# Mamba block with expert gate on one core: another way to the layer-norm roots in the first stage, another order at its start

## What is computed

```python
def _layernorm(x, axis=-1, eps=1e-05):
    m = jnp.mean(x, axis=axis, keepdims=True)
    v = jnp.var(x, axis=axis, keepdims=True)
    return (x - m) / jnp.sqrt(v + eps)
...
xn = _layernorm(x)
x = xn @ Wx.T
z = xn @ Wz.T
x = jax.nn.silu(_causal_conv(x, conv_w, conv_b))
b, c = x @ Wb.T, x @ Wc.T
dt = jax.nn.softplus(x @ Wdt.T + b_dt)
y = _ssd_scan(x, b, c, dt, a) + d_param * x
s = (groupnorm(y) * silu(z)) @ Wout.T
g = silu(experts(xn))          # router: softmax(xn @ Wr + br), top 1024 tokens of each expert
out = x_input + s * g
```

## Time and profile before

| | us |
|---|---|
| median of 3 runs | 1302.14 (1301.19 to 1302.91) |
| the profiled execution | 1301.87 |
| its span, first to last instruction | 1300.1 |

### The profile page before, as it was taken

The page is one execution under the profiler, slowest core; times in us unless marked ns, Lnnn a source line. Parts: engine busy times, 40 slices in busy tenths (PEclk is TensorE's granted clock), DMA queues, the critical chain, the costliest instruction groups (busy, mean ns, idle before and its releaser), DMA issues.

```text
span 1300.1 us, 26491 instructions
## 1 busy us (share of the span) xinstructions
PE 1267.4 (97%) x10300; PEld 1058.3 (81%) x10300; DVE 935.5 (72%) x1877; ACT 634.7 (49%) x1302; POOL 775.8 (60%) x685
## 2 busy tenths in 40 slices
PE   6889999999999999999999999899999999999999
PEld 4556667888888888888888887699899989899998
DVE  7888676777756567567667657798677766787786
ACT  5888996433444443334333443444343332555554
POOL 3778865434444565567666545456666654577774
PEclk9999899999999999999999999899999999999999
DMA  8465355743544344354444444375454545777884
GB/s 280 141 240 209 124 211 171 149 147 135 155 146 166 128 133 155 134 173 138 149 137 154 139 147 143 131 209 114 91 115 88 97 87 117 224 256 255 267 267 155
DMA packets 121276, 210.55 MB, mean 162 GB/s; under 512 B 18368, under 2 KB 91712, under 8 KB 112832
## 3 DMA queue, kind: packets, MB, share of 16 engines
q1 hardware_dynamic: 107568, 191.67, 45.2%
q0 software_dynamic: 12288, 17.05, 7.7%
q10 hardware_dynamic: 1296, 0.15, 0.1%
HBM read 140.93 MB, written 67.90 MB: 161 GB/s over the span
## 4 chain that ended last, share of the span: by engine, by line
PE 81%; POOL 6%; DVE 5%; issue 3%; ACT 3%; DMA 2%; SPq 0%; POOLq 0%; ACTq 0%; DVEq 0%
PE ps L1125 22%; PE ps L1464 10%; PE ps L1721 9%; PE ps L1944 7%; PE ps L1923 7%; PE ps L1180 4%; PE ps L1249 4%; PE ps L527 2%; PE ps L1261 2%; PE ps L1212 2%; POOL acc L479 2%; PE ps L1195 2%; PE ps L1229 2%; PE ps L569 2%; DVE acc L227 1%
## 5 line engine op out<-in xcount | busy, mean ns | idle before, releaser
L1092 ACT ACTIVATE decay<-tap,ncum 128x128 f32<-128x128 f32 x344 | 105.4, 389 | 144.7 <-POOL tap L1005 144.5
L1649 POOL DMA_INDIRECT ffn_dram<-ob,idx x64 | 109.8, 1716 | 83.1 <-DVE ob L1568 68.8
L1683 ACT ACTIVATE mid<-ps,b_up 128x512 f32<-128x512 f32 x96 | 65.9, 688 | 154.3 <-PE ps L1464 152.5
L1034 POOL TENSOR_SCALAR yb<-x,dcol 128x512 f32<-128x512 f32 x64 | 45.2, 708 | 154.4 <-DMA y_dram<-yb 96.1
L924 DVE TENSOR_TENSOR yb<-ps,yb 128x256 f32<-128x256 f32 x128 | 48.4, 420 | 123.0 <-PE ps L1261 118.9
L1011 POOL TENSOR_TENSOR x_lo<-x,x_hi 128x512 fp32r<-128x512 f32 x56 | 75.0, 1340 | 81.0 <-ACT x_hi L1078 80.9
L1022 POOL TENSOR_TENSOR c_dec<-cT,ecum_row 128x512 f32<-128x512 f32 x64 | 87.1, 1361 | 34.0 <-PE ps L1261 23.8
L479 POOL TENSOR_TENSOR acc<-acc,tap 128x512 f32<-128x512 f32 x64 | 82.0, 1286 | 36.4 <-DVE acc L227 35.5
L1125 PE MATMUL ps<-x_hi,w_hi_c 128*128 128x512 f32 x240 | 99.6, 415 | 0.0
L1125 PE MATMUL ps<-x_hi,w_hi_b 128*128 128x512 f32 x240 | 99.5, 415 | 0.0
L1806 POOL TENSOR_SCALAR yc<-yc,gn_scale,gn_shift 128x512 f32<-128x512 f32 x56 | 88.2, 1587 | 16.6 <-DMA yc<-y_dram 16.5
(11 more groups left out here) (305 smaller groups left out, 4070.5 us busy)
## 6 DMA issues: line engine op xcount, KB each, us to landing
tap<-cum_dram SPq DMA_DIRECT2D x43, 512.0 KB, 5.1
x_dram<-x SPq DMA_DIRECT2D x16, 1024.0 KB, 5.1
x<-x_dram SPq DMA_DIRECT2D x16, 1024.0 KB, 6.0
ecum_row<-ecum_dram SPq DMA_DIRECT2D x128, 128.0 KB, 3.0
y_dram<-yb SPq DMA_DIRECT2D x16, 1024.0 KB, 7.5
yc<-y_dram SPq DMA_DIRECT2D x16, 1024.0 KB, 6.2
cum_row<-cum_dram SPq DMA_DIRECT2D x21, 512.0 KB, 5.5
ring<-in_x SPq DMA_DIRECT2D x16, 512.0 KB, 8.1
```

Of the source, the lines that this page charges most:

```text
L1092: n = nc.scalar.activation(decay[g % 2][:, h, :], cum_row[g % NR][:, h, :], ACT.Exp, bias=t.ncum[:, g, h:h + 1])
L1649: pool.indirect_dma_start(out=t.ffn_dram, out_offset=bass.IndirectOffsetOnAxis(ap=t.idx[:, e, h * HC + c:h * HC + c + 1], axis=0), in_=ob[ ...
```

## The change

Six edits, all in the front.

1. **Groups and roots.** The groups become blocks 0, 1, 2, 3, and then 4 to 6, 7 to 9, 10 to 12, 13 to 15. For the first four ACT's Sqrt, DVE's reciprocal and DVE's 4-step `polish` stay, all ahead of ACT's one change to the Silu table. For the others `root` makes the inverse root on DVE alone: a start value by an integer shift, a multiply and an add, then Newton steps, 13 dependent instructions on 128x12 values. Steps 0 to 6 stand at the end of passes 0, 3, 6 and 9, steps 7 to 12 behind `lo_part` in passes 1, 4, 7 and 10. POOL's `polish` and the three late `deviation`s are gone; POOL waits for the 13th step ahead of blocks 4, 7, 10 and 13.
2. **Statistics** run one block less ahead (block b + 6 in pass b, to pass 9).
3. **First loads.** Block 0 comes in two halves; block 1 is issued once the second half has landed; the identity (128 columns of the constants) comes first on ACT's queue, the rest of the constants behind block 1; four small tensors move from ACT's queue to SP's, behind block 7 and ahead of the first store.
4. **Start of the chain.** Block 0 is normalized and turned chunk by chunk (`first_turn`). `deviation(0)` stands ahead of the high part of `wx`, which is made in two halves; DVE makes half of its low part, POOL the other half ahead of block 1. `turn(1)` stands behind all four projections of block 0.
5. **Zeros.** PE runs 26 matmuls on a tile of zeros from the start and 3 more behind `first_turn` (`keep_busy`).
6. DVE, ACT and POOL wait for the late small tensors near the end of the front.

The diff, cut to its core:

```diff
-    GROUPS = ((0, 1), (1, 2), (2, 4), (4, 8), (8, 12), (12, 16))
-    EARLY = 2
+    GROUPS = ((0, 1), (1, 2), (2, 3), (3, 4), (4, 7), (7, 10), (10, 13), (13, 16))
+    EARLY = 4
...
+    WARM, WARM_HI = 26, 3
+    SECOND = (1, 4, 7, 10)
...
                 if c == 0:
                     dve.wait_ge(x_loaded[b % NX], 16 * (b // NX + 1))
+                elif (b, c) == (0, 2):
+                    dve.wait_ge(half_loaded, 16)
                 n = v.bn_stats(stat6[:, CH * b + c, :], xin[b % NX][:, c, :])
                 if c < CH - 1:
...
+            def root(g, first, end):
+                lo, hi = GROUPS[g]
+                n, cols, base = CH * (hi - lo), slice(CH * lo, CH * hi), STEPS * (g - EARLY) + 4 * EARLY + 1 + CH
+                raw, a, y = var[:, 0:n], sq[:, 0:n], rstd[:, cols]
+                for i in range(first, end):
+                    if i == 0:
+                        dve.wait_ge(var_done, hi)
+                        step = v.tensor_scalar(raw, moment[:, cols, 1], EPS, None, ALU.add)
+                    else:
+                        dve.wait_ge(norm_step, base + i)
+                        if i == 1:
+                            step = v.tensor_scalar(a.bitcast(I32), raw.bitcast(I32), 1, None, ALU.arith_shift_right)
+                        elif i == 2:
+                            step = v.tensor_scalar(y.bitcast(I32), a.bitcast(I32), -1.0, float(MAGIC), ALU.mult,
+                                                   ALU.add)
+                        elif i == STEPS - 1:
+                            step = v.scalar_tensor_tensor(nmr[:, cols], moment[:, cols, 0], -1.0, y, ALU.mult,
+                                                          ALU.mult)
+                        elif i % 3 == 0:
+                            step = v.tensor_tensor(a, raw, y, ALU.mult)
+                        elif i % 3 == 1:
+                            step = v.scalar_tensor_tensor(a, a, -0.5, y, ALU.mult, ALU.mult)
+                        else:
+                            step = v.scalar_tensor_tensor(y, a, 1.5, y, ALU.add, ALU.mult)
+                    step.then_inc(norm_step, 1)
...
-                    n = v.tensor_scalar(xn[0][:, c, :], xin[0][:, c, :], rstd[:, c:c + 1], nmr[:, c:c + 1],
-                                        ALU.mult, ALU.add)
-                n.then_inc(xn_ready, 1)
+                    v.tensor_scalar(xn[0][:, c, :], xin[0][:, c, :], rstd[:, c:c + 1], nmr[:, c:c + 1],
+                                    ALU.mult, ALU.add).then_inc(norm_step if c < CH - 1 else xn_ready, 1)
...
+            v.memset(zeros, 0.0)
             v.memset(warm[:, :], EPS).then_inc(norm_step, 1)
             block_stats(0)
             inverse(0)
             polish(0)
...
             dve.wait_ge(wx_hi_done, 1)
-            v.tensor_tensor(wx_lo[:, :, :], wx[:, :, :], wx_hi[:, :, :].bitcast(F32), ALU.subtract).then_inc(
-                wx_lo_done, 1)
-            block_stats(1)
+            v.tensor_tensor(wx_lo[:, 0, :], wx[:, 0, :], wx_hi[:, 0, :].bitcast(F32), ALU.subtract).then_inc(norm_step, 1)
+            stats(1, 0)
...
                 lo_part(0, k)
+            for c in range(1, CH):
+                stats(1, c)
             inverse(1)
             polish(1)
-            block_stats(2)
...
                     conv(b + 1, m)
-                    if m == 1 and b + 2 < NB:
+                    if b == -1 and m in (0, 2):
+                        block_stats(2 + m // 2)
+                        inverse(2 + m // 2)
+                        polish(2 + m // 2)
+                    if m == max(0, min(b + 1, 1)) and b + 2 < NB:
                         for k in range(KT):
                             lo_part(b + 2, k)
-                    if b == -1 and m < 3:
-                        block_stats(3 + m)
-                    elif b == 0 and m < 2:
-                        block_stats(6 + m)
-                    elif b >= 1 and b + 7 < NB:
-                        stats(b + 7, m)
-                    if b == -1 and m == 0:
-                        inverse(2)
-                if b in (0, 4, 8):
-                    inverse(3 + b // 4)
+                        if b in SECOND:
+                            root(EARLY + b // 3, HALFWAY, STEPS)
+                    if b == -1 and m == 3:
+                        block_stats(4)
+                    elif b == 0 and m in (0, 2):
+                        block_stats(5 + m // 2)
+                    elif b >= 1 and b + 6 < NB:
+                        stats(b + 6, m)
+                if b + 1 in SECOND:
+                    root(EARLY + (b + 1) // 3, 0, HALFWAY)
             thin_copy(NB - 2)
             thin_copy(NB - 1)
...
+            act.dma_start(t.ident, ins["const"][:, C_ID:C_ID + P]).then_inc(ident_loaded, 16)
             for dst, src in smalls:
                 act.dma_start(dst, src).then_inc(small_loaded, 16)
...
+            deviation(0)
             act.wait_ge(wx_loaded, 16)
-            nc.scalar.activation(wx_hi[:, :, :], wx[:, :, :], ACT.Copy).then_inc(wx_hi_done, 1)
-            deviation(0)
+            for k in range(KT):
+                nc.scalar.activation(wx_hi[:, k, :], wx[:, k, :], ACT.Copy).then_inc(wx_hi_done, 1)
             for k in range(KT):
                 hi_part(0, k)
-            deviation(1)
...
                 if b == -1:
-                    deviation(2)
+                    deviation(1)
...
+                if b == -1:
+                    split(0, 2)
+                    deviation(2)
                 if b + 2 < NB:
                     for k in range(KT):
...
-                    split(b + 1, 2)
+                    if b >= 0:
+                        split(b + 1, 2)
                     split(b + 1, 3)
+                    if b == -1:
+                        deviation(3)
                 else:
+                    act.wait_ge(late_loaded, 16 * len(lates))
                     nc.scalar.activation(a_pos[:, :, :], t.rows[:, 0:1, :], ACT.Exp).then_inc(sca, 1)
                     thin_evict(b + 1)
...
-                if b in (0, 4, 8):
-                    deviation(3 + b // 4)
...
-            def polish(g):
-                lo, hi = GROUPS[g]
...
-                gp.tensor_scalar(neg[:, 0:n], moment[:, cols, 0], -1.0, 0.0, ALU.mult, ALU.add).then_inc(norm_step, 1)
...
-                pool.wait_ge(norm_step, first + 3)
...
-                pool.wait_ge(norm_step, first + 7)
             def layer_norm(b):
-                if b == 1:
...
+                if b < EARLY:
+                    pool.wait_ge(norm_step, 4 * (b + 1) + 1 + CH)
                 elif b in [lo for lo, _ in GROUPS]:
-                    polish(group_of(b))
+                    pool.wait_ge(norm_step, STEPS * (group_of(b) - EARLY + 1) + 4 * EARLY + 1 + CH)
...
+            pool.wait_ge(wx_hi_done, KT)
+            pool.wait_ge(xn_ready, 1)
+            nc.gpsimd.tensor_tensor(wx_lo[:, 1, :], wx[:, 1, :], wx_hi[:, 1, :].bitcast(F32),
+                                    ALU.subtract).then_inc(wx_lo_done, 1)
             layer_norm(1)
...
+            def keep_busy(n):
+                for _ in range(n):
+                    pe.matmul(ps_x[MT - 1][:, :], zeros[:, 0:P], zeros, start=True, stop=True)
+            def first_turn():
+                for c in range(CH):
+                    pe.wait_ge(*((norm_step, 6 + c) if c < CH - 1 else (xn_ready, 1)))
+                    for k in range(KT):
+                        mm = pe.transpose(ps_t[k][:, c * P:(c + 1) * P], xn[0][:, c, k * P:(k + 1) * P], t.ident)
+                        if c == CH - 1:
+                            mm.then_inc(xnT_ready, 1)
...
-            pe.wait_ge(cst_loaded, 16)
-            turn(0)
-            pe.wait_ge(wx_lo_done, 1)
+            pe.wait_ge(norm_step, 1)
+            keep_busy(WARM)
+            pe.wait_ge(ident_loaded, 16)
+            first_turn()
+            keep_busy(WARM_HI)
             for b in range(-1, NB - 1):
                 project(b + 1, 0)
                 project(b + 1, 1)
-                if b + 2 < NB:
+                if 0 <= b < NB - 2:
                     turn(b + 2)
                 project(b + 1, 2)
                 project(b + 1, 3)
                 if b == -1:
+                    turn(1)
                     pe.wait_ge(small_loaded, 16 * len(smalls))
                 thins(b + 1)
+                if b == 0:
+                    pe.wait_ge(cst_loaded, 16)
                 if b >= 0:
                     sum_thins(b)
...
-            load_x(0)
+            sp.dma_start(xin[0][:, 0:2, :], x_blk[0][:, 0:2, :]).then_inc(x_loaded[0], 16)
+            sp.dma_start(xin[0][:, 2:CH, :], x_blk[0][:, 2:CH, :]).then_inc(half_loaded, 16)
             sp.dma_start(wx[:, :, :], ins["wx"].rearrange("(k p) n -> p k n", p=P)).then_inc(wx_loaded, 16)
-            sp.dma_start(t.cst[:, :], ins["const"]).then_inc(cst_loaded, 16)
-            for b in range(1, NX):
+            sp.wait_ge(half_loaded, 16)
+            load_x(1)
```

(27 more changed lines are left out.)

21 lines of the change are left out of this document (4 added, 17 removed).

## The result

| | before | after |
|---|---|---|
| median, 8 runs each on one chip | 1301.10 (1300.15 to 1302.91) | 1297.74 (1296.11 to 1299.89) |
| the profiled execution | 1301.87 | 1298.12 |
| its span | 1300.1 | 1296.3 |

The ratio is 0.9973, 95% interval 0.9964 to 0.9982: 3.4 us less by the medians (3.5 by the ratio), where the forecast was 10 us less and its range ended at 1297.0. The sign was right, the size was not.

The account below looks back on a forecast made before the run. It took the front to be bound by a POOL-DVE ring of 9.50 us a block, PE needing 9.44, plus stalls. Start 3.0 + stalls 11.8 - roots 6.0 + 1.8 - 0.5 = 10.1 us, giving 1292.0 us; range 1287.5 to 1297.

Parts of the forecast that it names:

- How much of it shows?: Roots on DVE: first half adds 0.8 to 0.9 us, second 1.1 to 1.2; 2.0 a group, 6.0 for three.
- The 5 us until the full pace: Start, PE: with zeros from about 1.1 us on, full pace after some 5 us, an estimate with upper end 9.
- The store of block 0: Start: POOL's layer_norm(2) waits for this store, expected to land at 21.7 instead of near 20.7; turn(2) needs the result at 24.
- the sum: Gain at POOL's layer_norm(13): start 3.0 + stalls 11.8 - roots 6.0 = 8.8 us; then + 1.8 and - 0.5, 10.1 us.
- both stalls: Ahead of blocks 8 and 12, around ACT's Sqrt and table loads: 5.9 us each, 11.8 us in all, forecast to go.
- the pitch of a step: DVE's small dependent root steps: 0.20 us each, lower bound less than 0.18, upper 0.30.
- the second half: Last 6 root steps ahead of the third conv: 1.2 us on DVE, POOL stands 1.1 to 1.2 us ahead of layer_norm.
- PE's lag: At block 13 PE was 1.8 us late from its spell at the lower clock; without the stall it should not arise.
- the terms + 1.8 and - 0.5: Behind layer_norm(13): PE's lag gone gives 1.8 us; POOL's fullest block (9.9 us) gives 0.5 back.
- should reach the end whole: Behind the front the program is untouched and PE sets its time, so the front's gain or loss carries through.
- The steps cost more: Rival, root steps on DVE: 0.30 us each or waits not overlapping, 52 x 0.1 = 5.2 us, 1297; chance 0.14.
- slower than before: Rival, root on DVE: steps over 0.39 us eat the whole 10.1 us; at 0.45 us, 1305; chance 0.03.

Follow-up runs that it names:

- e1: The changed kernel with POOL's weight splits moved to passes 1, 2, 4, 5, 7, 8, 10, 11, away from the roots' first halves; ratio to before 0.9960.
- e6c: The changed kernel with the third Newton step left out of the late groups' root, 10 steps instead of 13; ratio to before 0.9947.
- e3: The changed kernel without the 29 matmuls on zeros; ratio to before 0.9979.
- e4: The changed kernel with block 0, the constants and the small tensors loaded whole by the queues of before; ratio to before 0.9969.
- e5c: The changed kernel with only its start kept: blocks 4 to 15 use ScalarE's Sqrt and GpSimd's steps in groups of four again; ratio to before 1.0005.
- e7c: The changed kernel with e1's moved splits, e4's loads and a root of 12 steps, eps added within the Newton steps; ratio to before 0.9938.
- e8c: The kernel of e7c with 18 matmuls on zeros ahead of the first block instead of 26; ratio to before 0.9937.

## Why the prediction was wrong, and where it was right

**The step that failed is "How much of it shows?"** It took 0.8 to 0.9 us for a root's first half (7 x 0.20 less the 0.54 of DVE's wait) and so 2.0 us for a root, where the rows show 3.41. Two of the seven steps wait for POOL's instruction: 0.62 - 0.17 = 0.45 us for the first, 1.22 - 0.17 = 1.05 for the shift. 2.0 + 0.45 + 1.05 = 3.5 us, against 3.41 measured, and e1 (without the 1.05) has 2.36 where 2.0 + 0.45 = 2.45. Three roots: 3 x 1.41 = 4.2 us. The prediction did look at what POOL does for DVE there (it ends DVE's wait), not at what POOL's running instruction does to DVE's own.

The same wait took 1.1 us more in pass 0 and 0.55 in the `polish` of block 3:

```profile
23.54 2.52 POOL L507 TENSOR_TENSOR acc<-acc,tap 128x512 f32<-128x512 f32 x2
25.15 0.18 DVE L184 RECIPROCAL inv<-dev 128x4 f32<-128x4 f32 x1 [0.37 <-ACT dev L377]
25.36 0.71 DVE L192 SCALAR_TENSOR_TENSOR stat_t<-moment,inv 128x4 f32<-128x4 f32 x1
...
40.36 1.30 POOL L507 TENSOR_TENSOR acc<-acc,tap 128x512 f32<-128x512 f32 x1 [1.10 <-DVE acc L263]
40.39 1.29 DVE L217 TENSOR_SCALAR stat_t<-stat_t 128x12 int32<-128x12 int32 x1
...
53.45 1.30 POOL L527 TENSOR_TENSOR w_lo_b<-cT,w_hi_b 128x512 fp32r<-128x512 f32 x1
53.52 0.19 DVE L251 TENSOR_REDUCE tap<-edge 128x12 f32<-128x36 f32 x1 [0.55 <-POOL acc L507]
```

**Not every small operation waits.** In these rows GpSimd's instruction runs to 26.06 and to 54.75. The reciprocal at 25.15 and the reduction of `edges` at 53.52 start and end within it at their usual 0.18 and 0.19 us, although they too read and write SBUF; the `polish` step behind the reciprocal stands until 26.07. The forms seen to wait are TENSOR_SCALAR, SCALAR_TENSOR_TENSOR and TENSOR_TENSOR with all their tensors in SBUF. This bears on the prediction: against dear steps it set the 0.18 us of a reciprocal and the 0.19 us of this reduction, and a single row of a form that does not wait is no price for one that does.

**The trace of before could have shown it**, in another stage. Before, at the change from scan to experts:

```profile
801.91 1.11 POOL L1005 TENSOR_SCALAR_AFFINE_SELECT tap<-tap 128x1024 f32<-128x1024 f32 x1
802.34 2.22 DVE L872 TENSOR_TENSOR state<-state,dec 128x256 f32<-128x256 f32 x1
802.97 1.29 POOL L1022 TENSOR_TENSOR c_dec<-cT,ecum_row 128x512 f32<-128x512 f32 x1
```

The same product of two tensors in SBUF takes 0.41 us in the trace after, with POOL idle beside it:

```profile
811.28 0.41 DVE L931 TENSOR_TENSOR state<-state,dec 128x256 f32<-128x256 f32 x1
```

In the front of before DVE's large operations of the convolution read PSUM with at most one operand tensor in SBUF. Of its small ones ten reductions of `edges` (0.19 us each) and 40 BN_AGGR run wholly inside an instruction of POOL at their usual length, and the `polish` steps, of a form that does wait, met POOL at rest. So the front's rows alone were silent, and even pointed the other way.

**The start: near, with its parts wrong.** `conv(0, 0)` was forecast at 15.4, came at 14.40 in the profiled execution, and at 14.71 and 15.54 in e6c and e1, which have the same start. Their 26 zeros lasted 7.24, 7.40 and 8.38 us: zeros that last longer hold the first transposes back. The 5 us until the full pace, for which the prediction had no row, would have made them last 8.1. Block 2's first `conv` was forecast near 42.5 and came at 42.86: 1.0 us better at its beginning, 1.6 us of waits for POOL behind that. The zeros are worth about 0.5 us and the split loads nothing that shows (e3, e4). The store of block 0 came as priced: `layer_norm(2)` starts at 21.39 behind it, forecast 21.7. And e5c shows that the gain lasts only because the group at block 4 no longer needs block 7: the start and the roots can't be added as two independent terms, as the sum did.

The start, PE, ACT and DVE of the kernel after:

```profile
5.80 0.30 ACT L377 ACTIVATE dev<-moment,warm 128x4 f32<-128x4 f32 x1 [3.57 <-DVE moment L173]
7.14 1.39 DVE L235 TENSOR_SCALAR xn<-ring,rstd,nmr 128x256 f32<-128x256 f32 x4
8.28 1.04 PE L551 MATMUL ps<-cst,xn 128*128 128x128 f32 x8
...
10.23 0.40 PE L576 MATMUL ps<-xn_hi,wx_lo 128*128 128x512 f32 x1
...
42.86 0.74 DVE L255 SCALAR_TENSOR_TENSOR acc<-ps,cw,acc 128x511 f32<-128x511 f32 x1
```

**Right:** both stalls are gone; the pitch of a step, 0.20 us; the second half, for which POOL waits 1.16 us (forecast 1.1 to 1.2); and PE's lag. Its last transposing, before and after:

```profile
171.12 1.03 PE L515 MATMUL ps<-cst,xn 128*128 128x128 f32 x8
```

```profile
166.14 1.03 PE L560 MATMUL ps<-cst,xn 128*128 128x128 f32 x8
```

4.98 us at block 15, 1.3 more than at block 13: the terms + 1.8 and - 0.5.

**The account** at `layer_norm(13)`: 8.8 - 4.2 (three roots) - 1.6 (pass 0 and block 3) + 1.0 (start) = 4.0, measured 3.65. One more term was too large: the stalls were taken at 11.8 us, but before, the eight turns from block 5 to block 13 last 87.42 us, only 11.2 more than eight turns of 9.53, as those behind a stall are shorter (9.43 and 9.11). In parts: block 5 gains 2.7 us (2.4 by these terms), the turns from there to block 13 gain 0.9 (1.0 by these terms), where the sum had 3.0 and 5.8. Behind block 13 another 1.3 comes from PE, and 1.3 is lost again by the first matmul of the experts (PE, before and after):

```profile
822.95 0.47 PE L1464 MATMUL ps<-xg_hi,up_hi 128*128 128x512 f32 x1
```

```profile
819.30 0.47 PE L1523 MATMUL ps<-xg_hi,up_hi 128*128 128x512 f32 x1
```

3.65 us are left, and the end has 3.8. PE's lead does not shrink evenly: it is 4.7 us in the first half of the scan and 5.4 near its end (the same matmuls at 777.13 before, 771.72 after), and the loss falls into the change from scan to experts. From the start of the scan's last projection to the first matmul of the experts before takes 16.9 us, after 17.3, e1, e3 and e4 15.8, e6c 17.9, e7c 17.7, e8c 15.5, with the same instructions. From PE's last transposing to the end of the program before takes 1128.9 us, after 1130.2, e1 1127.6, e7c 1130.0: differences of up to 2.6 us between these executions do not come from the front. DVE's and POOL's instructions meet differently there (the rows at 802 us above). That the same wait for POOL makes this difference fits the rows, but no run tested it; this part stays open. The prediction's sentence that the front's gain "should reach the end whole" was 1 us too hopeful.

Of the rivals none names this cause. "The steps cost more" gave nearly the time (1297), through a pitch of 0.30 us that the trace refutes, so that its nearness is luck; "slower than before" had the right sentence, a step that costs more than 0.39 us, but for all 52 of them, where seven do.

## What to carry to other kernels

When work moves onto VectorE, look at what GpSimd executes at that moment, not only at who waits for whom: elementwise arithmetic on SBUF, even on twelve columns, can stand until GpSimd's instruction is over, so small dependent steps belong where GpSimd is idle, or GpSimd's large independent work belongs elsewhere. Take the price of a step from a row of the same form that meets the same neighbour: here the reciprocal and the reduction did not wait and the steps did. Look for a row of the same form of instruction with two very different times in any stage of the trace; that is where such a wait shows, for in these profiles it stands as busy time of VectorE (84 of 100 us before, 95 after) and not as idle time. And if one part of a change lets the next one start early, ask what the next one needs besides: a gain ahead of a wait for something else is given back.
